# Router products of a transformer kernel: 128 columns wide in place of 8, with zero-padded weights

## Chip, cores and metric

The kernel runs on one core of a Trainium2 chip. The metric is the device time of one execution in microseconds, the median of several runs. TensorE (PE) has two clock levels, 1.2 and 2.4 GHz; the profile gives the granted clock as a share of 2.4 GHz (1.00 or 0.50, or a mean of both).

## What is computed

Four blocks, each followed by a residual sum and a layer norm: a wave-field attention, an FP4 feed-forward layer, a windowed attention, and a mixture of experts. The change lies in the router of the last block:

```python
def _L1_ffn_ref(x, Wr, Wg, Wu, Wd, Sg, Su, Sd): 
    xt = x.reshape(T, H)
    scores = softmax(xt @ Wr, axis=-1)               # Wr: 256 x 8
    topk_w, topk_idx = top_k(scores, 2)
    topk_w = topk_w / (topk_w.sum(-1, keepdims=True) + EPS)
    ...                                              # the two experts of each token, and a shared one
    return out + shared
```

Here x has 4 x 1024 tokens, so T = 4096: 32 tiles of 128 tokens (NT), or 8 chunks of 512 (NCH). A token has D = 256 channels, which are KD = 2 blocks of 128.

## The kernel before

All five engines run an order written out by hand, with semaphores between them. The part around the change comes after the windowed attention. `X` holds all tokens in SBUF, with a token in each partition; the router needs channels in the partitions. So for each chunk c of four tiles:

- `rows_transposed(c)` (PE, L1823): 8 transposes of 128x128 put the chunk into two PSUM banks, 0 and 1 or 4 and 5 in turn, and count up `d_rt`. It waits for `c_ln`, the layer norm of the chunk.
- `rows_copied(c)` (ACT, L577): one copy of 128x1024 from PSUM to `rx[:, c % 2]`. It waits for `d_rt` and for the products of chunk c - 2, and counts up `d_rx`.
- `logits(c)` (PE, L1831): for each of the four tiles w and each of the two channel blocks k a product in full fp32, tokens of `rx` as the stationary operand (128x128), the router's weights `wrr[:, k]` as the moving one. The profile shows each of these 8 products as two loads of weights and two matmuls, so 16 records for a chunk and 128 in all. The result of tile t goes to columns 8t to 8t + 7 of PSUM bank 6. The last product of a chunk counts up `d_lg`.

The order on PE is products of chunk c, transposes of chunk c + 2, products of chunk c + 1, and so on:

```python
            pe.wait_ge(d_ld, 16)
            for c in range(NCH):
                logits(c)
                if c + 2 < NCH:
                    rows_transposed(c + 2)
```

The transposes of chunks 0 and 1 stand earlier, among the last products of the attention. On ACT the copies of chunks 2, 3 and 4 come first, then `normalise_chunk(7)` (L552, the last layer norm of the attention), then the copies of chunks 5, 6 and 7.

When `d_lg` has reached 8, DVE reads the 256 columns of bank 6 at once (L1367), and with ACT and PE finds the two experts of each token and its place among the expert's tokens (L1367 to L1437). Two small PE products take part in this (L1858, L1859). Then POOL scatters the tokens to DRAM by expert, 64 indirect transfers (L861), while PE, ACT and DVE work on the shared expert for half of the chunks (`shared`, L1546 to L1548 in the trace). When all tokens are out, the tiles of the experts follow (`tile`, again L1546 to L1548, L1891, L1907), 71 of them, then a gather (L878) and the last layer norm.

L1546 to L1548 are the three matmuls of the helper `three`, which makes a product from high and low parts in fp32r. The router doesn't use it.

The weights `wrr` are loaded by SP's queue (L315), between two loads of expert weights: the shared expert's (L314) and expert 0's (L316). PE waits for them with `d_ld` ahead of `logits(0)`.

Of the kernel before, what the change touches and what calls it, by code (L numbers as in the profile page):

```python
# [12 lines left out]
P = 128  # L13
# [4 lines left out]
KD = D // P  # L18
# [21 lines left out]
E = 8  # L40
# [35 lines left out]
def build(nc, cst, xT, x, wqkvgT, wave_cols, bias_cols, coupling_rows, woutT, bout, wgu_rows, wd_rows, wqk_T, wo_rows, bo, wr, experts, out):  # L76
    ctx = ExitStack()
    with ctx:
        place = {"at": 0, "top": 0}

        def sb(name, shape, dt=F32):
            size = 2 if dt == BF16 else 4
            for s in shape[1:]:
                size *= s
            t = nc.alloc_sbuf_tensor_at(name, shape, dt, offset=base + place["at"])
            place["at"] += (size + 31) // 32 * 32
            place["top"] = max(place["top"], place["at"])
            return t
# [6 lines left out]
        PS = ctx.enter_context(nc.psum_tensor("PS", [P, 8, 512], F32))  # L95
# [87 lines left out]
        rx = sb("rx", [P, 2, KD, CH])  # L183
# [20 lines left out]
        SWh, SWl = sb("SWh", [P, EW], F32R), sb("SWl", [P, EW], F32R)  # L204
        raw_at = place["at"]
        raw = sb("raw", [P, 2, EW])
        wrr = sb("wrr", [P, KD, E])
        pos = sb("pos", [P, 2, NT], mybir.dt.int32)
        gate = sb("gate", [P, 2, NT])
        of_tile = sb("of_tile", [P, NE + 1], mybir.dt.int32)  # L210
# [1332 lines left out]
        def _(pe):  # L1543
# [282 lines left out]
            def logits(c):  # L1826
                pe.wait_ge(d_rx, c + 1)
                for w in range(4):
                    for k in range(KD):
                        at = (4 * c + w) * E  # L1830
                        mm = pe.matmul(PS[:, 6, at:at + E], rx[:, c % 2, k, w * P:(w + 1) * P], wrr[:, k], start=k == 0, stop=k == KD - 1)  # L1831
                mm.then_inc(d_lg, 1)

            scores(NCH - 1, 1)
# [7 lines left out]
# [4 lines that stand above are left out]
# [115 lines left out]
def constants():  # L1961

    import numpy as np
    c = np.zeros((P, C_END), np.float32)
    c[:, C_ID:C_ID + P] = np.eye(P)
    c[:, C_IOTA:C_IOTA + CH] = np.arange(CH)
    i, j = np.arange(P)[:, None], np.arange(2 * P)[None]
    c[:, C_CAUSAL:C_CAUSAL + 2 * P] = np.where(j >= i + P + 1, -1e30, 0.0)
    c[:, C_CHAN:C_CHAN + HD] = np.arange(P)[:, None] % HD == np.arange(HD)
    c[:, C_HALF:C_EPS] = -0.5  # L1970
    c[:, C_EPS:C_TRI] = EPS
    c[:, C_TRI:C_ONE] = np.arange(P)[:, None] < np.arange(P)[None]
    c[:, C_ONE:C_DOWN] = 1.0
    c[:, C_DOWN:C_END] = E - np.arange(E)
    return c


def layout(**a):

    import numpy as np  # L1980

    def by_channel(w):
        return np.ascontiguousarray(w.reshape(-1, P, w.shape[-1]).transpose(1, 0, 2))

    def expert(g, u, d):
        return np.concatenate([by_channel(w).reshape(P, -1) for w in (g, u, d)], 1)

    def whole_tiles(w):
        return np.concatenate([w, np.zeros((FFP - FF, w.shape[1]), w.dtype)])

    def heads(v):
        return np.repeat(v, HD).reshape(KD, P).T

    x = np.asarray(a["L0_attn_x"]).reshape(T, D)
    cols = np.stack([heads(np.asarray(a["L0_attn_wave_" + n])) for n in ("frequency", "damping", "phase")], 1)
    return dict(
        cst=constants(),
        xT=by_channel(x.T),
        x=np.ascontiguousarray(x.reshape(NT, P, D).transpose(1, 0, 2)),
        wqkvgT=by_channel(np.asarray(a["L0_attn_Wqkvg"]).T),  # L2000
        wave_cols=np.ascontiguousarray(cols),
        bias_cols=np.ascontiguousarray(np.asarray(a["L0_attn_bqkvg"]).reshape(8, P).T),
        coupling_rows=by_channel(np.repeat(np.asarray(a["L0_attn_field_coupling"]), HD, axis=0)),
        woutT=by_channel(np.asarray(a["L0_attn_Wout"]).T),
        bout=np.asarray(a["L0_attn_bout"]).reshape(1, D),
        wgu_rows=np.ascontiguousarray(np.stack([by_channel(whole_tiles(np.asarray(a["L0_ffn_" + n]))).reshape(P, 2 * FFP)
                                                for n in ("w_gate", "w_up")], 1)),
        wd_rows=by_channel(whole_tiles(np.asarray(a["L0_ffn_w_down"]).T).T).reshape(P, 2 * FFP),
        wqk_T=np.ascontiguousarray(np.stack([by_channel(np.asarray(a["L1_attn_w_qkv"])[:, j * D:(j + 1) * D].T) for j in range(2)], 1)),
        wo_rows=by_channel(np.asarray(a["L1_attn_w_out"])),  # L2010
        bo=np.asarray(a["L1_attn_b_out"]).reshape(1, D),
        wr=by_channel(np.asarray(a["L1_ffn_Wr"])),
        experts=np.ascontiguousarray(np.stack([expert(*(np.asarray(a["L1_ffn_" + n])[e] for n in ("Wg", "Wu", "Wd"))) for e in range(E)]
                                              + [expert(*(np.asarray(a["L1_ffn_" + n]) for n in ("Sg", "Su", "Sd")))])),
    )
# [20 lines left out]
```

## Time and profile before

| | |
|---|---|
| Median of 3 runs | 1209.07 us (1208.1 to 1212.84) |
| Profiled execution, its own time | 1211.1 us |
| Its span | 1209.3 us |
| Mean granted clock of TensorE | 0.928 |
| PE busy | 1052.5 us, 87% of the span |
| DVE, ACT, POOL busy | 790.2, 462.7 and 444.3 us |
| Products of the router (L1831) | 128 records, first start 597.7, last 630.1 us |

How to read it: the page says what share of the span each engine is busy and which chain of work ended last. A share over the whole span mixes stages; what a stage is worth is read from the views of that stage, above all the chain of waits in order of time, and the table of stretches, which has the granted clock of each.

### The profile page before, as it was taken

The numbers are of one execution on the slowest core, as the hardware profiler recorded it, in microseconds if no ns is written. First come the engines' busy times: TensorE is split into PE (matmuls) and PEld (weight loads), VectorE is DVE, ScalarE is ACT, GpSimd is POOL, SyncE is SP. The second block draws the span as 40 slices with busy tenths as digits, with TensorE's granted clock in tenths as the row PEclk, the third lists the DMA queues.
The fourth block names the chain that finished last, engine by engine and source line by source line (L and its number), as shares of the span: only waits on it lengthen the run. The fifth ranks groups of instructions, "written<-read, shape, count | busy, mean of one in ns | idle before, by whom it ended". The sixth has DMA issues, their size and how long they took to land.

```text
span 1209.3 us, 19343 instructions
## 1 busy us (share of the span) xinstructions
PE 1052.5 (87%) x5976; PEld 927.6 (77%) x5977; DVE 790.2 (65%) x1336; ACT 462.7 (38%) x790; POOL 444.3 (37%) x357
## 2 busy tenths in 40 slices
PE   5789972589999999998985987999999999998872
PEld 4567752589999998998884876888888888887762
DVE  7978899699999987787716443444444444443676
ACT  5726432234444444666522232222332232222225
POOL 3302003134444446322104777244413430005764
PEclk9989985699999999999856998999999999998996
DMA  6110020900000000200101221333223121112324
GB/s 273 36 35 1 1 78 1 319 20 1 0 0 0 0 1 1 105 2 1 54 0 48 102 100 61 108 104 104 85 71 105 60 100 53 56 44 78 102 81 168
DMA packets 42387, 77.30 MB, mean 64 GB/s; under 512 B 5474, under 2 KB 32868, under 8 KB 40932
## 3 DMA queue, kind: packets, MB, share of 16 engines
q1 hardware_dynamic: 24532, 40.52, 9.3%
q0 software_dynamic: 7008, 26.22, 6.6%
q10 hardware_dynamic: 10800, 9.94, 2.8%
q8 instruction: 28, 0.46, 0.2%
q14 instruction: 19, 0.16, 0.0%
HBM read 45.47 MB, written 31.20 MB: 63 GB/s over the span
## 4 chain that ended last, share of the span: by engine, by line
PE 54%; DVE 13%; POOL 11%; DVEq 9%; issue 8%; ACT 3%; DMA 1%; POOLq 1%; ACTq 0%
PE PS L1546 14%; PE PS L1548 13%; PE PS L1547 13%; POOL tokens_by_expert L861 5%; POOL gathered L878 5%; PE PS L1907 3%; PE PS L1670 2%; DVEq L1093 2%; PE PS L1831 2%; DVEq L1198 2%; PE PS L1575 2%; PE PS L1891 1%; DVE hx L1105 1%; PE PS L1588 1%; DVEq L1210 1%
## 5 line engine op out<-in xcount | busy, mean ns | idle before, releaser
L1490 DVE TENSOR_TENSOR hb<-PS,gs 128x512 f32<-128x512 f32 x71 | 49.1, 691 | 153.0 <-ACT gs L644 153.0
L1546 PE MATMUL PS<-EWs,xeh 128*128 x284 | 118.9, 419 | 1.2 <-DVE xel L1484 1.2
L1548 PE MATMUL PS<-EWs,xel 128*128 x284 | 112.0, 394 | 0.0
L1547 PE MATMUL PS<-EWs,xeh 128*128 x284 | 111.6, 393 | 0.0
L1546 PE MATMUL PS<-WGh,bxh 128*128 128x352 f32 x256 | 88.4, 345 | 19.9 <-DVE hv L1192 13.6
L878 POOL DMA_INDIRECT gathered<-expert_outputs,pos x64 | 62.5, 977 | 115.8 <-DMA expert_outputs<-ye 96.4
L644 ACT ACTIVATE gs<-PS 128x512 f32<-128x512 f32 x71 | 42.5, 599 | 159.3 <-PE PS L1548 159.3
L852 POOL TENSOR_TENSOR EWs<-raw,zrow 128x3072 fp32r<-128x3072 f32 x7 | 47.6, 6805 | 151.1 <-PE PS L1548 151.0
L1670 PE MATMUL PS<-WD,htf 128*128 128x256 f32 x384 | 88.5, 380 | 1.6 <-ACT htf L468 1.5
L861 POOL DMA_INDIRECT tokens_by_expert<-X,pos x64 | 64.2, 1004 | 65.1 <-DVE pos L1437 45.9
L1546 PE MATMUL PS<-EWs,heh 128*128 x284 | 85.7, 302 | 1.6 <-DVE hel L1494 1.6
L1547 PE MATMUL PS<-WGl,bxh 128*128 128x352 f32 x256 | 85.5, 334 | 0.0
L1548 PE MATMUL PS<-WGh,bxl 128*128 128x352 f32 x256 | 85.4, 334 | 0.0
L1494 DVE TENSOR_TENSOR hel<-PS,heh 128x512 fp32r<-128x512 f32 x71 | 49.1, 692 | 48.0 <-ACT heh L649 48.0
L1548 PE MATMUL PS<-EWs,hel 128*128 x284 | 80.4, 283 | 0.0
L1547 PE MATMUL PS<-EWs,heh 128*128 x284 | 79.7, 281 | 0.0
L1670 PEld LDWEIGHTS PS<-WD,htf 128*128 128x128 f32 x384 | 71.2, 190 | 10.9 <-ACT htf L468 2.5
L649 ACT ACTIVATE heh<-PS 128x512 fp32r<-128x512 f32 x71 | 42.5, 599 | 90.7 <-PE PS L1907 90.7
L1546 PE MATMUL PS<-xh,WQh 128*128 128x512 f32 x128 | 53.7, 420 | 20.0 <-DVE WQl L928 13.2
L1546 PEld LDWEIGHTS PS<-WGh,bxh 128*128 128x128 f32 x256 | 50.5, 197 | 23.7 <-issue 14.8
L1546 PEld LDWEIGHTS PS<-EWs,xeh 128*128 128x128 f32 x284 | 53.7, 189 | 14.2 <-issue 1.6
L1548 PEld LDWEIGHTS PS<-EWs,xel 128*128 128x128 f32 x284 | 53.7, 189 | 10.7
(331 smaller groups left out, 3077.1 us busy)
## 6 DMA issues: line engine op xcount, KB each, us to landing
raw<-experts POOLq DMA_DIRECT2D x6, 1536.0 KB, 7.1
tokens_by_expert<-zrow SPq DMA_DIRECT2D x1, 9088.0 KB, 29.4
xe<-tokens_by_expert ACTq DMA_DIRECT2D x71, 128.0 KB, 2.0
expert_outputs<-ye SPq DMA_DIRECT2D x71, 128.0 KB, 1.7
raw<-experts SPq DMA_DIRECT2D x3, 1536.0 KB, 6.2
xraw<-xT SPq DMA_DIRECT2D x8, 512.0 KB, 5.2
X<-x SPq DMA_DIRECT2D x1, 4096.0 KB, 16.8
y<-X SPq DMA_DIRECT2D x8, 512.0 KB, 2.6
```

The lines of the kernel that those rows point to most:

```text
L644: act.activation(gs[:, h], PS[:, 2], ACT.Silu).then_inc(e_si, 1)
L649: act.activation(heh[:, h].rearrange("p a c -> p (a c)"), PS[:, 4 + h], ACT.Copy).then_inc(e_hhi, 1)
L852: pool.tensor_tensor(hi, src, zrow[:, :].unsqueeze(1).to_broadcast([P, EW // D, D]), ALU.add)
L861: pool.indirect_dma_start(out=XS, out_offset=bass.IndirectOffsetOnAxis(ap=pos[:, j, t:t + 1], axis=0), in_=X[:, t], in_offset=None).then_i ...
L878: pool.indirect_dma_start(out=gathered[c][:, j, t], out_offset=None, in_=YS, in_offset=bass.IndirectOffsetOnAxis(ap=pos[:, j, 4 * c + t:4 ...
L1490: dve.tensor_tensor(hb[:, h], PS[:, 3], gs[:, h], ALU.mult).then_inc(e_hb, 1)
L1494: dve.tensor_tensor(hel[:, h].rearrange("p a c -> p (a c)"), PS[:, 4 + h], heh[:, h].rearrange("p a c -> p (a c)").bitcast(F32), ALU.subtr ...
L1546: pe.matmul(out_, wh, vh, start=first, stop=False)
L1547: pe.matmul(out_, wh, vl, start=False, stop=False)
L1548: return pe.matmul(out_, wl, vh, start=False, stop=last_)
L1670: mm = pe.matmul(PS[:, 7, i * D:(i + 1) * D], htf[:, i, k], WD[:, k], start=k == 0, stop=k == FT - 1)
L1907: t = pe.transpose(PS[:, 4 + h, j * P:(j + 1) * P], hb[:, h, j * P:(j + 1) * P], ident)
```

## The change

The router's weights are stored and loaded 128 columns wide; columns 8 to 127 are zeros. Each product is 128 columns wide. The result of tile t goes to columns 8t to 8t + 127 of bank 6; tile t + 1, which comes later, starts eight columns further on and overwrites the zeros of tile t from there, its first product with `start=True`. After the last tile the first 256 columns hold what they held before. The last tile ends at column 8 x 31 + 128 = 376 of the bank's 512.

```diff
-        wrr = sb("wrr", [P, KD, E])
+        wrr = sb("wrr", [P, KD, P])
...
                     for k in range(KD):
                         at = (4 * c + w) * E
-                        mm = pe.matmul(PS[:, 6, at:at + E], rx[:, c % 2, k, w * P:(w + 1) * P], wrr[:, k], start=k == 0, stop=k == KD - 1)
+                        mm = pe.matmul(PS[:, 6, at:at + P], rx[:, c % 2, k, w * P:(w + 1) * P], wrr[:, k], start=k == 0, stop=k == KD - 1)
...
-        wr=by_channel(np.asarray(a["L1_ffn_Wr"])),
+        wr=np.concatenate([by_channel(np.asarray(a["L1_ffn_Wr"])), np.zeros((P, KD, P - E), np.float32)], 2),
```

The number of instructions and their order are the same on every engine. `wrr` grows from 64 to 1024 bytes of each partition, and its load from 8 to 128 KB.

## Rows read from the trace of the kernel before

**Rows 1.** The page, parts 1 and 2: PE's busy time, and granted clock in 40 slices.
```profile
PE 1052.5 (87%) x5976; PEld 927.6 (77%) x5977; DVE 790.2 (65%) x1336; ACT 462.7 (38%) x790; POOL 444.3 (37%) x357
PEclk9989985699999999999856998999999999998996
```
**Rows 2.** Chain that ended last, 597.7 to 630.6: start us, us, what.
```profile
597.82 1.68 PE PS L1831 x16
599.50 0.93 PE PS L1823 x8
600.43 1.69 PE PS L1831 x16
602.12 1.67 PE PS L1823 x8
603.79 3.21 PE PS L1831 x16
607.00 1.80 PE PS L1823 x8
...
623.84 6.64 PE PS L1831 x32
630.51 0.42 DVE rt L1367
```
**Rows 3.** Stretches: length; busy us of PE, PEld, DVE, ACT, POOL; clock; DMA.
```profile
596.00:600.00 4.00, 4.00 (x38) 4.00 (x37) 2.93 (x8) 2.27 (x5) 0.00 (x0) 1.00 0.01 2
600.00:602.00 2.00, 2.00 (x21) 2.00 (x19) 1.91 (x9) 1.02 (x1) 1.16 (x2) 1.00 0.00 0
603.00:630.30 27.30, 27.30 (x132) 27.30 (x130) 0.00 (x0) 7.08 (x9) 0.28 (x2) 0.50 0.00 0
```
**Rows 4.** Waits, 590 to 700: total us, times, longest us.
```profile
POOL tokens_by_expert L861 <- DVE pos L1437: 45.9, 1, 45.9
DVE rt L1367 <- PE PS L1831: 28.4, 1, 28.4
```
**Rows 5.** Timeline of PE: fp32 products 256 wide and what follows; last product ahead of the router.
```profile
301.71 2.76 PE L1670 MATMUL PS<-WD,htf 128*128 128x256 f32 x12
304.31 0.82 PE L1663 MATMUL PS<-C,hq 128*128 128x128 f32 x6
...
597.55 0.27 PE L1548 MATMUL PS<-Zh,PTl 128*128 128x256 f32 x1
```
**Rows 6.** Timeline of ACT, 609 to 615: last layer norm, and a copy to rx.
```profile
609.76 2.06 ACT L552 ACTIVATE X<-X,cnm,crs 128x256 f32<-128x256 f32 x4
613.85 1.02 ACT L577 ACTIVATE rx<-PS 128x1024 f32<-128x1024 f32 x1 [2.03 <-PE PS L1823]
```
**Rows 7.** Timeline of POOL, 600 to 604: what that layer norm waits for.
```profile
603.22 0.20 POOL L816 TENSOR_TENSOR cnm<-cnm,crs 128x4 f32<-128x4 f32 x1
```
**Rows 8.** Chain that ended last: first scatter (of 64), and end of the last.
```profile
649.32 1.20 POOL tokens_by_expert L861
...
731.77 2.40 DMA tokens_by_expert<-X,pos
```
**Rows 9.** Timeline of PE, 736 to 743 and 1095 to 1101: from idle to full clock.
```profile
736.36 0.66 PE L1891 MATMUL PS<-C,xe 128*128 128x128 f32 x2 [4.63 <-DMA xe<-tokens_by_expert]
738.22 0.79 PE L1546 MATMUL PS<-EWs,xeh 128*128 x1 [1.20 <-DVE xel L1484]
...
742.16 0.40 PE L1546 MATMUL PS<-EWs,xeh 128*128 x1
...
1095.13 0.80 PE L1546 MATMUL PS<-DTh,SWh 128*128 128x512 f32 x1 [0.52 <-DVE ye L1502]
...
1100.41 0.43 PE L1546 MATMUL PS<-DTh,SWh 128*128 128x512 f32 x1
```
**Rows 10.** Load of the router's weights: issue times of L315, and time to landing.
```profile
L315 SPq DMA_DIRECT2D wrr<-wr x1: 432/432/432, 492.1 to 492.1; - x1
...
DMA to landing us min/median/max: 6.0/6.0/6.0
```

## The prediction

> **What bounds the kernel now.** I read the page first. PE is busy for 87% of the span [rows 1], but the line of the granted clock under it counts for more here: it stands at 9 in most slices and falls to 5 and 6 in two places, and the later one, slices 21 and 22 of 30.2 us each, covers 605 to 665 us. The router lies at its start. The chain that ended last comes next, in order of time [rows 2]: from 597.82 to 630.48 us it is PE and nothing else, the router's products (L1831) and the transposes for them (L1823) in turn, until DVE starts on the finished logits at 630.51. DVE had stood idle for 28.4 us for them [rows 4], and POOL, whose 64 scatters come after the routing, for 45.9 us [rows 4]. So here a microsecond of PE is a microsecond of the kernel.
>
> What sets PE's pace in this stage? The same 16 records take 1.69 us at 600.43 and 3.21 us at 603.79 [rows 2]; 8 transposes take 0.93 us before and 1.80 us after. The work is the same, the clock isn't: 1.00 from 600 to 602 us, 0.50 from 603 to 630.3 us [rows 3], though PE and its loads are busy without a break in both. What PE did before the clock fell was 5 us of products with 8 moving columns and transposes, and it went on with that for 27 us at 1.2 GHz. Ahead of them, with products of 256 columns up to 597.55 [rows 5], it was at 2.4 GHz [rows 3].
>
> Second: what does a product of 8 columns cost? 1.69 / 16 = 0.106 us a record at the full clock, though 8 columns are next to nothing to stream. What fills the time is the load of 128x128 new weights that each record needs. The low clock gives 3.21 / 16 = 0.201 us.
>
> **The change, part by part.** *Width of the products.* Nothing is added or moved on PE; 128 records get 128 columns in place of 8. I need the price of such a record at the full clock, which the trace doesn't have. It has neighbours. Below: fp32 records of 256 columns start 12 in 304.31 - 301.71 = 2.60 us, 0.217 us each [rows 5]; half the columns is 0.108 us, and the 8-column record can't be beaten: 0.106 us. Above: a transpose, also a load of 128x128 and 128 columns, 0.93 / 8 = 0.116 us [rows 2]. I take 0.112 us, between the two, since each resembles it in one thing (the type of product, the width). So 120 more columns cost 0.006 us a record, or 128 x 0.006 = 0.8 us in all, because the stream runs beside the next record's load.
>
> That "beside" carries the forecast. If a load had to wait for the stream before it, the 256-column records would take 0.217 + 0.106 us; they take 0.217 [rows 5], all of it stream. The Trainium skill speaks against it: "TensorE: Matmul & The Clock Gate", section "What overlaps and what doesn't", has loads overlap with matmuls in flight only where their row groups differ, and here all 128 rows are used by both. By that rule the stage would cost 32.9 us, as worked out under the rival "in turn", and the gain would be gone. The row is a measurement of this kernel, so I go by it.
>
> *The clock.* With 128 columns a product keeps the array streaming nearly all of its time, as the products ahead of 597 us did. I expect the clock to stay at 2.4 GHz through the stage. Then the stage is 8 chunks x 16 x 0.112 = 14.3 us of products and 6 x 0.93 = 5.6 us of transposes, 19.9 us. Before it was 1.68 + 0.93 + 1.69 + 1.67 + 4 x (3.21 + 1.80) + 6.64 = 32.65 us [rows 2] (the pair of 3.21 and 1.80 stands there four times). The gain is 12.7 us: 8.5 from products, 4.2 from transposes that the change doesn't touch. With the ends of the price it is 13.5 us (0.106) and 12.2 us (0.116).
>
> *Who else must keep up.* At the faster pace the copies on ACT may be late next. One takes 1.02 us [rows 6]; it may start when its transposes are done and must be ready when the products of the chunk between are, 1.79 us later, so some 0.7 us are left with the handshakes. The long one in the queue is the last layer norm, 2.06 us, which ACT runs after the copy of chunk 4 [rows 6]; its input is there at 603.4 us [rows 7]. In the new time the products start at 597.8, those of chunk 3 at about 606.0 and of chunk 5 at about 611.4; the copy of chunk 4 ends at 607.0, the layer norm at 609.1, the copy of chunk 5 at 610.1. The transposes of chunk 7, which need that layer norm, come at 613.2. The tightest point, the copy of chunk 7, has 0.7 us to spare. Cost: nothing; without that cover each late copy would cost its lateness, under 1 us.
>
> *Wider load of the weights.* 128 KB in place of 8 in SP's queue at 492.1 us, 6.0 us to landing before [rows 10]. PE needs it at 597.7, 99 us later; expert 0's weights behind it are used after 731 us. A microsecond more is hidden. If it weren't, it would be 1 us, as an estimate from the landing times. The padded tile in SBUF moves its neighbours by 960 bytes, which costs no time.
>
> *What follows.* The routing on DVE, the scatter (649.32 to 734.2 us [rows 8]) and the experts start 12.7 us earlier and last as long. Nothing fixed in time stands on the path: POOL waits for the routing alone, and PE waited 4.63 us for the scattered tokens after its share of the work [rows 9]. PE is idle during the routing with or without the change, so I credit nothing to the clock there. How long PE stays at 1.2 GHz after a pause does vary: dense work began at 738.22 and was at full pace by 742.16, 3.9 us; in the tail 1095.13 and 1100.41, 5.3 us [rows 9]. Half of such a difference is time, so about 1 us either way that has nothing to do with the change.
>
> **The sum.** 1211.1 - 12.7 = 1198.4 us for an execution like the profiled one. That one was 2.0 us over the median, so the median should be 1209.07 - 12.7 = 1196.4 us. With the price (0.5 up, 0.8 down), 1 us of clock, and 1 to 2 us by which runs of one kernel differ, the likeliest case spans 1193.5 to 1199.5 us.
>
> **The rivals.**
> *It falls all the same.* The clock drops at 602 us as before, because the zeros or the transposes in between count for it, not the width. For it: I can't see in this trace what the clock reacts to; in the low stretch, a third of the time went to 128-column transposes and it didn't rise. Against it: the spell of transposes and 256-column products before 597 us held it. Price: 128 columns at half clock take 0.217 us by rows 5 and up to 1.80 / 8 = 0.225 us by rows 2, against 0.201 us for 112 of the 128 records at most. That is 1.8 to 2.7 us lost: 1211.3 us. Chance 0.13.
>
> *It falls for part of the stage.* The transposes are over a quarter of the new stage and break up the products, so the clock may drop and rise again, as it does after pauses elsewhere. Each microsecond of work at full clock takes two then. With a quarter to three quarters of the gain lost, 3 to 9 us are left: 1203 us as the middle. Chance 0.08. The Trainium skill has a rule for this, the same page's section on "PE-mode transpose": transposes don't count as a busy PE and don't bring the full clock. The low stretch agrees as far as it goes; the held clock ahead of 597 us, mixed with products, can't tell.
>
> *In turn.* This ends on the other side. Place: each of the 128 records, if a load of fp32 weights can't run beside a stream and rows 5 hide the load in some other way. At full clock a record is 0.106 + 0.108 = 0.214 us, the stage 27.3 + 5.6 = 32.9 us, no change: 1209.4 us. From the point where the clock falls too it decides: 0.201 + 0.217 = 0.418 us a record, 8 x 16 x 0.418 = 53.5 us and 9.8 for the transposes, 30.6 us slower: 1239.7 us. Against it: rows 5. Chance 0.04, of which 0.03 with the low clock.
>
> *The gain is given back behind the stage.* Had the path from 649 us been bound by something with its own start, the 12.7 us would turn into waiting there. The chain shows POOL released by the routing [rows 4], so this has hardly any chance, and I count it with the others.
>
> **How the numbers follow.** The clock holds: 0.75. Falls for part: 0.08. Falls as before: 0.13. In turn: 0.04. A measurement of this kernel can tell about 0.5%, 6 us, from no change. Faster by over that (under 1203.0 us): 0.75 and, of the part-time case, 0.05, in sum 0.80. Within: 0.13, the 0.01 of in turn at full clock and the other 0.03 of the part-time case, 0.17. Slower: 0.03. The range starts at 1193.5 us and has to reach beyond the likeliest case, whose edges leave out about 0.03; up to 1206 us it takes in the part-time case, 0.72 + 0.08 = 0.80.
>
> **What would show it.** The granted clock from 600 to 618 us: 1.00 if I am right, 0.50 from 603 us if the clock reacts to something else. Sixteen products in 1.7 to 1.9 us in every chunk; 3.4 us with the clock at 1.00 would be loads and streams in turn. Transposes at 0.93 us in all six places. DVE's wait for the logits down from 28.4 to about 15.7 us, and L1367 starting at about 617.8. The distance from there to the first scatter (18.8 us) and from the first scatter on unchanged. Idle time of PE between products would mean late copies. Wrong would be a time of 1206 us or more, or the right time with a stage that isn't 12 to 14 us shorter.

## The result, and the profile after

The changed kernel takes 1195.97 us (median of 4 runs, 1193.71 to 1198.0), the kernel before 1210.66 us in its 4 runs. The ratio is 0.988 with a 95% interval of 0.9856 to 0.9903: 11.7 to 17.4 us less. The forecast was 1196.4 us.

The chain that ended last, in the changed kernel, stands here beside [rows 2] (start us, us, what):

```profile
593.91 1.78 PE PS L1831 x16
595.70 0.87 PE PS L1823 x8
596.57 1.79 PE PS L1831 x16
598.36 0.87 PE PS L1823 x8
599.23 1.79 PE PS L1831 x16
...
609.00 0.87 PE PS L1823 x8
609.87 3.59 PE PS L1831 x32
613.48 0.42 DVE rt L1367
```

Sixteen records take 1.78 to 1.80 us in every chunk, the last two chunks included. Before they took 1.69 and then 3.21 us. The transposes take 0.87 us in all six places; before they took 0.93, then 1.67 where the clock fell, then 1.80. The stage ends with the start of L1367 at 613.48 us, 19.57 us after it began; before it was 630.51 - 597.82 = 32.69 us. So it is 13.1 us shorter.

The stretches of the changed kernel give the reason, beside [rows 3] (the columns are the same):

```profile
593.90:603.00 9.10, 9.10 (x85) 9.10 (x84) 4.12 (x14) 3.57 (x5) 2.36 (x4) 1.00 0.01 3
603.00:613.40 10.40, 10.40 (x95) 10.25 (x93) 0.00 (x0) 4.87 (x7) 0.00 (x0) 1.00 0.00 0
613.40:617.00 3.60, 0.05 (x1) 0.00 (x0) 2.66 (x7) 1.70 (x2) 0.00 (x0) 1.00 0.00 0
619.00:622.30 3.30, 0.00 (x0) 0.00 (x0) 2.85 (x8) 0.00 (x0) 0.00 (x0) 0.50 0.00 0
```

PE is busy all of the stage, as before, but the clock stays at 2.4 GHz to its end and falls only in the idle time behind it. The waits of the stage answer to [rows 4]:

```profile
POOL tokens_by_expert L861 <- DVE pos L1437: 32.7, 1, 32.7
DVE rt L1367 <- PE PS L1831: 15.2, 1, 15.2
```

DVE's wait for the logits is 13.2 us shorter, and POOL's for the routing 13.2 us as well.

**The other part of the difference between the profiles.** The spans differ by more than the stage, 1209.3 - 1192.3 = 17.0 us. The stage already begins 3.9 us earlier (593.91 against 597.82), and that isn't the change's doing. Transposes of the attention, long before the router, start 3.5 us earlier too. Here is that line's summary in the kernel before, then in the changed one (behind the durations the first and last start):

```profile
L1721 PE MATMUL PS<-C,X x64: 272/272/273, 461.0 to 558.2; 128*128 128x128 f32 x64
```
```profile
L1721 PE MATMUL PS<-C,X x64: 272/272/273, 457.5 to 554.7; 128*128 128x128 f32 x64
```

Up to there both kernels run the same instructions. What differs visibly is how the clock fell in the first 260 us, where PE waits often. Here are the stretches from 120 to 140 and from 240 to 260 us, before and after (PE alone: length, busy, clock, DMA):

```profile
120.00:140.00 20.00, 17.89 (x69) 0.91 0.00 0
240.00:260.00 20.00, 16.61 (x98) 0.91 0.18 62
```
```profile
120.00:140.00 20.00, 17.90 (x73) 1.00 0.00 0
240.00:260.00 20.00, 14.95 (x98) 1.00 0.11 37
```

As an estimate, a mean of 0.91 over 20 us is 3.6 us at half clock and 1.8 us of time if PE is busy then; two such stretches would account for the 3.5 us. From 160 to 180 us it is the other way round (0.83 before, 0.74 after), in a stretch where PE is idle for a third of the time. No run isolates the cause.

Which executions get the earlier start doesn't follow the change. The fourteen profiles of this study begin the router's products at 593.7 to 598.1 us. The changed kernel itself began them at 593.91 us in one profile and at 595.92 in another (after_again), and load_only, which has its padded tile and its load, at 598.06. One profiled execution can thus flatter a change by 4 us, which is a third of this gain. The medians of several runs are less exposed to it.

Behind the stage the two traces are equally long: from the start of L1367 to the end of the span 578.8 us in both (1209.3 - 630.5, 1192.3 - 613.5). That they agree so closely is chance: in the other profiles without a fill behind the stage the same part takes 578.7 to 581.6 us.

### The profile page after: what moved, and what is told of

It reads as the page before. It is cut to its first block, busy times and chain, and to the rows that moved or that the text cites. A ratio compares the mean times of both kernels' runs of the same rounds, so it can differ in the third digit from the quotient of the medians.

```text
span 1192.3 us, 19343 instructions
## 1 busy us (share of the span) xinstructions
PE 1034.9 (87%) x5976; PEld 908.1 (76%) x5977; DVE 788.0 (66%) x1336; ACT 462.4 (39%) x790; POOL 446.1 (37%) x357
## 4 chain that ended last, share of the span: by engine, by line
PE 66%; DVE 12%; issue 6%; POOL 6%; DVEq 6%; ACT 3%; POOLq 1%; DMA 1%; ACTq 0%
PE PS L1546 17%; PE PS L1548 16%; PE PS L1547 16%; POOL gathered L878 5%; PE PS L1670 5%; PE PS L1907 3%; PE PS L1575 2%; PE PS L1891 1%; PE PS L1831 1%; PE PS L1588 1%; PE PS L1663 1%; DVEq L1093 1%; ACT X L695 1%; DVEq L1106 1%; DVEq L1198 1%
## 5 line engine op out<-in xcount | busy, mean ns | idle before, releaser
L1546 PE MATMUL PS<-SWh,Hh 128*128 128x256 f32 x128 | 40.7, 318 | 25.5 <-DVE Hl L1464 25.5
```

Source lines behind the costliest of these rows:

```text
L1546: pe.matmul(out_, wh, vh, start=first, stop=False)
```

## Experiments

"Stage" is the time from the first product of the router to the start of L1367, from the chain (in narrow_fill from the first fill).

| | Median us (before) | Ratio, 95% | Stage us |
|---|---|---|---|
| load_only | 1209.09 (1209.76) | 0.9986, 0.9972 to 1.0001 | 32.65 |
| width_64 | 1198.43 (1209.76) | 0.9894, 0.9877 to 0.9911 | 19.23 |
| nonzero_pad | 1197.89 (1209.76) | 0.9890, 0.9873 to 0.9907 | 19.56 |
| narrow_fill | 1205.77 (1209.76) | 0.9963, 0.9946 to 0.9979 | 28.0 |
| width_32 | 1194.17 (1210.07) | 0.9875, 0.9850 to 0.9900 | 19.21 |
| width_256 | 1209.55 (1210.07) | 0.9994, 0.9974 to 1.0014 | 32.92 |
| transposes_in_gap | 1198.73 (1210.07) | 0.9906, 0.9874 to 0.9937 | 19.57 |
| warm_all | 1197.14 (1210.07) | 0.9892, 0.9865 to 0.9919 | 19.57 |
| after_again | 1196.73 (1211.23) | 0.9884, 0.9862 to 0.9905 | 19.57 |
| early_fill | 1196.06 (1211.23) | 0.9871, 0.9848 to 0.9894 | 19.57 |
| fills_width_32 | 1197.68 (1211.23) | 0.9885, 0.9861 to 0.9908 | 19.21 |
| width_16 | 1206.96 (1211.23) | 0.9961, 0.9944 to 0.9979 | 32.69 |

### Load and place without the width: load_only

```diff
-mm = pe.matmul(PS[:, 6, at:at + P], rx[...], wrr[:, k], ...)
+mm = pe.matmul(PS[:, 6, at:at + E], rx[...], wrr[:, k, 0:E], ...)
```

> The changed kernel's padded tile and its 128 KB load, but products 8 columns wide again. If the width of the products holds the clock (my theory): granted clock 0.50 from about 5 us after the stage's first product, stage 32.7 us from the first product to the start of L1367, and a time like before, 1209 to 1212 us. If the gain came from the other place of the tiles in SBUF or from the load: stage about 19.6 us and about 1196 us.

The stage is back at 32.65 us and the gain is gone. Two stretches of its trace (PE alone):

```profile
598.00:602.50 4.50, 4.50 (x43) 0.99 0.01 2
603.00:630.60 27.60, 27.60 (x133) 0.50 0.00 0
```

The padded tile and its load do nothing for the time that this run can show. The gain is the width of the products, and with it the clock.

### How wide: width_64, width_32, width_16

```diff
-mm = pe.matmul(PS[:, 6, at:at + P], rx[...], wrr[:, k], ...)
+mm = pe.matmul(PS[:, 6, at:at + 32], rx[...], wrr[:, k, 0:32], ...)
```

> The changed kernel with products 64 columns wide (same padded tile). A record costs the load alone, 0.106 us, if the stream lies beside it. If the clock holds: stage 8 x 16 x 0.106 + 7 transposes' shares of 0.87, about 19 us, and a time 0.7 us under the changed kernel's, 1195 us. If half the width is not enough to hold the clock all the way: 0.50 in the stage, about 32 us and 1209 us. A stage in between would be a clock that falls for a part of it.

> The changed kernel with products 32 columns wide. Clock held: stage about 19 us, 1195 us. Clock lost as with 8 columns: stage about 32 us, 1209 us.

> The changed kernel with products 16 columns wide. Twice 8, half of 32, and both outcomes are open: clock held, stage about 19 us and 1195 us; or lost as with 8 columns, stage about 32 us and 1209 us.

With 64 and with 32 columns the clock was 1.00 all through the stage. Two rows from each chain, of width_64 and then of width_32:

```profile
595.39 1.73 PE PS L1831 x16
597.12 0.88 PE PS L1823 x8
```
```profile
594.19 1.71 PE PS L1831 x16
595.89 0.91 PE PS L1823 x8
```

So a record costs 0.108 and 0.107 us against 0.112 with 128 columns and 0.106 with 8. Columns 32 to 127 cost 19.57 - 19.21 = 0.36 us of the stage. (The expectation for width_64 counts seven places of transposes; there are six. Its median came out at 1198.4 us, not at 1195.) In the profiled execution of width_16 the clock fell where it falls with 8 columns:

```profile
597.80:602.50 4.70, 4.70 (x43) 0.96 0.00 2
602.50:604.00 1.50, 1.50 (x9) 0.50 0.04 11
604.00:630.40 26.40, 26.40 (x126) 0.50 0.00 0
```

Its runs don't all look like that one: four of nine took 1202.9 to 1205.2 us, the others 1207.0 to 1212.7. Only the mean granted clock over the whole execution is on record for them: 0.934 or 0.935 in the four quicker ones and 0.928 to 0.932 in the others. In the changed kernel's runs it is 0.940 to 0.944. That fits a clock that held for a part of the stage in the quicker ones, but those executions left no trace, so it isn't shown. The median is 4.3 us under the kernel before, and the interval leaves out no change. So 16 columns lie between the two outcomes that I had expected. The medians of 64 and 32 columns, and of the changed kernel, lie 1194.2 to 1198.4 us; differences among them are within what the early part of the kernel scatters, and I don't rank them.

### Do zeros count for less: nonzero_pad

```diff
-wr=np.concatenate([by_channel(np.asarray(a["L1_ffn_Wr"])), np.zeros((P, KD, P - E), np.float32)], 2),
+wr=np.tile(by_channel(np.asarray(a["L1_ffn_Wr"])), (1, 1, P // E)),
```

> The changed kernel with the router's weights repeated 16 times in place of the zeros; columns 8t + 8 and on of a tile are overwritten by the next ones or not read. If only the columns streamed count: clock, stage (19.6 us) and time (1196 us) as in the changed kernel. If zeros count for less in what the clock reacts to: no difference either here, since it held with zeros; a higher power draw that lowered the clock would show as 0.8 or 0.5 in the stage.

A stage of 19.56 us at clock 1.00, against the changed kernel's 19.57. What the columns hold makes no difference here. That zeros are enough to hold the clock, the changed kernel had already shown.

### Is it the streaming, or the product's own width: narrow_fill

```diff
 for w in range(4):
+    pe.matmul(PS[:, 7, 0:CH], SWh[:, 0:P], SWh[:, 0:CH], start=True, stop=True)
     for k in range(KD):
         ...      # products 8 columns wide
...
 pe.wait_ge(d_ld, 16)
+pe.wait_ge(d_slo, 1)
 for c in range(NCH):
```

> The kernel before, products 8 columns wide, with one product of 512 columns in fp32r ahead of each tile's four records, into PSUM bank 7, which nobody reads: 32 of them. If streaming is what the clock reacts to: clock 1.00 throughout, stage 128 x 0.106 + 32 x 0.22 + 6 x 0.87 = 25.8 us in place of 32.7, so faster than before by about 7 us, 1202 to 1204 us. If the products' own width were what matters: clock 0.50, the fill costs 32 x 0.43 = 14 us on top, 1223 us.

The second added line waits for `SWh`, which the fill reads; the first fill starts right behind the attention's last product. The kernel does more work than before and takes 4 us less. For 25 us its narrow products ran at the full clock. Two rows of the chain show a tile's four records and the fill ahead of the next tile; then come stretches of PE alone:

```profile
595.95 0.34 PE PS L1832 x4
596.29 0.34 PE PS L1829
```

The clock fell in the last chunk. No transposes stand between the last two chunks:

```profile
595.70:616.00 20.30, 20.30 (x162) 1.00 0.01 1
...
620.00:621.00 1.00, 1.00 (x9) 0.81 0.00 0
621.00:623.60 2.60, 2.60 (x11) 0.50 0.00 0
```

I had expected 25.8 us, a clock of 1.00 throughout and 1202 to 1204 us. The stage was 28.0 us and the median 1205.8: a chunk with its transposes took 3.54 us, so at full clock the stage would have been 8 x 2.61 + 6 x 0.93 = 26.5 us, and the low clock at the end cost the other 1.5. The direction decides between the theories (with the clock at 0.50 throughout it would have been slower than before): products of the old width run at the full clock when wide ones stand between them. That it fell only after the transposes had ended suggests that they helped to hold it; no run with these fills and without transposes shows it.

### In turn or beside: width_256

```diff
-wrr = sb("wrr", [P, KD, P])
+wrr = sb("wrr", [P, KD, 2 * P])
...
-mm = pe.matmul(PS[:, 6, at:at + P], ...)
+mm = pe.matmul(PS[:, 6, at:at + 2 * P], ...)
```

> The changed kernel with weights padded to 256 columns and products 256 wide. If a load runs beside the stream of the record before: 0.217 us a record as in the fp32 products of the feed-forward layer, stage 27.8 + 5.2 = 33.0 us, 13.4 us more than the changed kernel, 1209 us, at clock 1.00. If load and stream took turns: 0.106 + 0.213 = 0.32 us a record, stage 46 us, 1222 us.

```profile
593.68 3.45 PE PS L1831 x16
597.14 0.87 PE PS L1823 x8
598.01 3.46 PE PS L1831 x16
```

A record takes 3.46 / 16 = 0.216 us, the stage 32.92 us at clock 1.00, both as expected for loads beside the stream; in turn would be 0.32 and 46. This fits the price that I read from [rows 5]. It also shows where padding stops to pay: at 256 columns the stream is the bound, and all that the clock gives is spent on zeros.

### Do transposes hold the clock: transposes_in_gap

```diff
+for i in range(76):
+    pe.transpose(PS[:, 7, i % 4 * P:(i % 4 + 1) * P], X[:, 0, 0:P], ident)
 pe.wait_ge(d_slo, 1)
 pe.wait_ge(d_oh, 1)
```

> The changed kernel with 76 further transposes of 128x128 right behind the last products, into bank 7, which nobody reads; they take 76 x 0.109 = 8.3 us of the 8.9 us in which PE waits for DVE's routing. If transposes keep the clock as products do: 1.00 to the end of the transposes, and a few us beyond. If they don't count (as a page of the notes has it): the clock falls to 0.50 some 5 us after the last product, in the middle of them; the 36 or so left then take twice as long, PE comes up to 4 us late to L1858, and the time grows by up to 4 us.

Timeline of PE (L1860 is L1858 of the changed kernel), and three stretches behind the last product:

```profile
613.53 8.46 PE L1857 MATMUL PS<-C,X 128*128 128x128 f32 x76
622.61 0.36 PE L1860 MATMUL PS<-ohr,tri 128*128 128x256 f32 x1 [0.62 <-DVE ohr L1394]
```
```profile
613.70:622.30 8.60, 8.30 (x76) 1.00 0.00 0
622.30:624.50 2.20, 1.35 (x10) 1.00 0.00 0
624.50:626.00 1.50, 0.00 (x0) 0.78 0.00 0
```

Nothing but transposes for 8.3 us, and the clock stays at 1.00, and still through the ten small records that follow up to 624 us; in the changed kernel, idle in the same place, it was at 0.50 from 619 us. The Trainium skill ("TensorE: Matmul & The Clock Gate", section "PE-mode transpose") says that the full clock doesn't engage for transposes, which don't count as a busy PE in the same way. These fp32 transposes held it, and the measurement decides. Whether transposes alone would bring the clock up from 1.2 GHz no run here shows. This kernel had only two runs, and its time says no more than "no slower than the changed kernel by much".

### Can the pauses be filled too: warm_all, early_fill, fills_width_32

The changed kernel leaves PE idle in the routing and starts the next stages at 1.2 GHz. These three fill pauses with 512-column products that nobody reads, for instance:

```diff
 pe.wait_ge(d_slo, 1)
+for i in range(36):
+    pe.matmul(PS[:, 7, 0:CH], SWh[:, 0:P], SWh[:, 0:CH], start=True, stop=True)
 pe.wait_ge(d_oh, 1)
```

early_fill has 20 of them ahead of the last `queries`, fills_width_32 has all five fills and products 32 wide. after_again is the changed kernel itself, for comparison.

> The changed kernel with products of 512 columns in fp32r, whose results nobody reads, in PE's pauses: 36 in the wait for the routing's first part, 36 in the wait for its second, 9 and 6 in the waits ahead of the first expert tile. Theory: PE keeps 2.4 GHz through the pauses. Shared expert starts at full clock (1.5 us less on PE, mostly hidden behind the scatter on POOL), first expert tile starts at full clock instead of 5 to 6 us at half: 2.5 to 3 us less on the path. In all 3 to 4 us under the changed kernel, 1192 to 1193 us. Rival: the fill is too long somewhere and delays the product behind it, or the path is held by POOL and DVE: no difference, or 1 to 2 us more.

> The changed kernel once more, as the measure for the two kernels with fills that run beside it: 1194 to 1198 us; in its profile the router stage at clock 1.00 and 19.6 us long.

> The changed kernel with 20 products of 512 columns (results unread) in PE's pause of 5.1 us before the queries of the last chunk, some 20 us ahead of the router, after which PE ran 4 to 5.5 us at 1.2 GHz. If the low clock there is on the path: those products at 2.4 GHz, 2 to 2.7 us earlier at the router, 1192 to 1195 us. If something else (the residual sums on DVE) bounds that place: the router stage begins no earlier and the time is the changed kernel's.

> All fills together (the early one, two in the routing, two ahead of the first expert tile) with products 32 columns wide. If the gains add: 2 to 2.7 us from the early fill, about 3 us behind the routing as the trace of warm_all shows, 0.3 us from the width: 1189 to 1192 us. If fills only move waiting about: 1194 to 1198 us, no difference from the changed kernel.

The fills raised the clock where they stood, with one exception. In warm_all the first dense products of the experts ran at the full clock; the same place in fills_width_32, where the pause came out longer (6.40 us waited at 722 us against 2.57), did not. First the stretches of warm_all, then of fills_width_32 (PE alone):

```profile
720.00:723.00 3.00, 0.74 (x5) 1.00 0.27 87
723.00:726.00 3.00, 3.00 (x14) 1.00 0.17 49
```
```profile
720.00:723.00 3.00, 0.76 (x3) 0.50 0.27 87
723.00:726.00 3.00, 3.00 (x8) 0.50 0.13 44
```

From L1367 to the end warm_all's trace takes 575.8 us, 3.0 less than the changed kernel's, as expected; but fills_width_32 takes 582.0. Another part of fills_width_32's loss lies ahead of that: PE's first expert transposes, which wait for the scattered tokens, started 107.6 us after L1367 there, 105.2 in warm_all and 105.5 in the changed kernel.

In early_fill the queries run at 2.4 GHz. First its stretch, then that of after_again:

```profile
572.00:578.00 6.00, 5.45 (x24) 1.00 0.44 145
```
```profile
572.00:578.00 6.00, 3.93 (x9) 0.59 0.73 262
```

From the start of the queries to the router's first product it takes 19.5 us, against 21.3 in the changed kernel. But from L1367 to the end early_fill's trace takes 580.8 us, against 578.8 and, in after_again, 579.4.

The medians show nothing of it: 1196.06 us for early_fill against 1196.73 for after_again beside it, 1197.68 for all together and 1197.14 for warm_all, with runs from 1191.3 to 1201.9. Of the fills that I hoped would add to 5 us, not one is distinguishable from the changed kernel. My hopes of 1192 to 1193 us for warm_all, 1192 to 1195 for early_fill and 1189 to 1192 for fills_width_32 were wrong. What eats the gain I can't say from these runs: the part behind L1367 alone scatters by 3 us without any fill. So no version beats the changed kernel by a margin that these runs can show.

## Why the prediction was right, and where it was off

**What bounds the stage.** PE alone, from the first product to L1367. Right: 13.1 us less on PE gave 13.2 us less waiting for DVE and POOL.

**Price of a record.** 0.112 us, taken between 0.106 and 0.116. Measured 1.79 / 16 = 0.112. The load beside the stream was the assumption that carried it; width_256 shows it directly. That the middle hit exactly is luck: the upper neighbour, 0.93 / 8, was itself too high, and with the 0.87 / 8 = 0.109 of transposes between wide products the measured price lies above both neighbours.

**Price of a transpose.** 0.93 us for eight was taken from the old stage; it is 0.87 between wide products. That is 0.4 us of the 6 places. The chain of the kernel before has this row as well, ahead of the stage:

```profile
593.85 0.87 PE PS L1823 x8
```

Where the chain draws the line between records and transposes shifts with the width. Sixteen records and eight transposes at the full clock take 2.61 us together with 8 columns (1.68 + 0.93), 2.62 with 32, 2.61 with 64 and 2.66 with 128. A likely reason is that the 0.93 included the first load behind narrow products; no run shows it. The forecast took its two prices from either side of that line, and for this alone its sum was 19.9 us and not 19.57.

**The clock.** It held. The reason given, that wide products keep the array streaming, is what load_only and narrow_fill bear out. That they do so nearly all of the time was more than was needed: with 64 and 32 columns the clock held as well. The rival "it falls all the same" had two grounds, zeros and transposes, and both have fallen: the changed kernel itself answers the first, transposes_in_gap the second. I had read it as a sign against the forecast that the transposes in the low stretch didn't bring the clock back. In that stretch they stood between narrow products, and this mixture is all that it speaks of.

**Falls for part of the stage.** It didn't happen in any of the six profiles with 128 columns, whose stages take 19.56 or 19.57 us. narrow_fill has the pattern, at its end, and the quicker runs of width_16 may have it.

**In turn.** Refuted by width_256, 0.216 us a record. This measurement also decides against the Trainium skill's rule that a load overlaps with a matmul only where the row groups differ ("TensorE: Matmul & The Clock Gate", "What overlaps and what doesn't"); here both use all rows.

**The copies on ACT.** No idle time of PE between products, as expected, and the layer norm came in time. Timeline of ACT in the changed kernel, beside [rows 6]:

```profile
601.93 1.02 ACT L577 ACTIVATE rx<-PS 128x1024 f32<-128x1024 f32 x1 [1.64 <-PE PS L1823]
602.85 2.06 ACT L552 ACTIVATE X<-X,cnm,crs 128x256 f32<-128x256 f32 x4
604.82 1.00 ACT L577 ACTIVATE rx<-PS 128x1024 f32<-128x1024 f32 x1
...
609.91 1.02 ACT L577 ACTIVATE rx<-PS 128x1024 f32<-128x1024 f32 x1 [1.64 <-PE PS L1823]
```

The copy behind the layer norm starts with no wait and ends at 605.8 us; the chunk's products start at 607.2. The last copy ends at 610.93 us and its products start at 611.66, so the tightest point had the 0.7 us to spare that were forecast.

**The wider load.** 6.3 us to landing in place of 6.0 [rows 10], long before its use. Hidden, as load_only confirms.

**What follows.** 18.8 us from L1367 to the first scatter (613.48 to 632.27), as before (630.51 to 649.32), and 578.8 us to the end in both. One thing I hadn't named: the scatter is no longer on the chain, which now goes through the shared expert's products. POOL's last scatter and PE's last shared product end within some 2 us of each other in both traces, so either can be the last; the first expert transposes start at 719.00 us, 105.5 us after L1367, against 105.9 before [rows 9].

**The size.** 12.7 us were forecast, and the stage gives 13.1. The medians differ by 14.7 us from the kernel before as measured beside them, and by 14.5 for after_again; the intervals reach down to 11.5. I can't say whether the 1.5 us beyond the stage are more than scatter. That the median met the forecast to 0.4 us is partly luck: the forecast started from 1209.07 us, and from the 1210.66 us measured beside the changed kernel the same 12.7 us lead to 1198.0.

## What to carry to other kernels

A TensorE that the profile shows as 100% busy can still run at half its clock, as it did here for 27 us of products 8 columns wide and transposes, each behind a new load of weights; read the granted clock of each stretch beside the busy time. Where each product needs new weights, as here, columns up to the time of the load cost almost nothing (0.106 us a record with 8, 0.112 with 128). So padding a narrow moving operand bought the full clock for everything in this stage, transposes included. Past the load's time it bought nothing: with 256 columns the stage was as long as before. Compare a stage by its own length in the two traces before crediting a difference of spans to the change.

## What the runs showed of the hardware that I had not expected

Pure transposes held the granted clock at 1.00 for 8.3 us. In the profiled executions it stayed at 1.00 with 32 columns a record and fell to 0.50 with 16, at the same 0.106 to 0.107 us a record at the full clock and with PE busy throughout in both. And two executions of the same instructions up to 461 us can differ by 3.5 us there; the granted clock of the stretches before differs too, and is the likely cause.
